# A gated attention and ternary feed-forward kernel: a new order of the calls in the lists of all five engines

## The reference

```python
xn = layernorm(x)                                   # over the last axis
# gated linear attention, 16 heads of 16
Q, K, V = (xn @ W.T).reshape(B, L, 16, 16)          # for each of Wq, Wk, Wv
g = clip(sigmoid(xn_heads @ gw.T), 1e-6)
Gc = exp(clip(cumsum(log(g), axis=1), -30, 30)) + 1e-6
R = silu(K @ sw.T)
S = cumsum(K V^T * R / Gc, axis=1) * Gc
attn = einsum(Q, S) @ Wo.T
# feed-forward with ternary weights and a low-rank side path
h = bitlinear(xn, w_fc) + gate * (xn @ v.T @ fast_b.T @ u.T)
ffn = bitlinear(relu(h) ** 2, w_proj)
out = x + attn + ffn
```

## Time and profile before

| | |
|---|---|
| median of 3 runs | 629.18 us (629.05 to 629.48) |
| span of the profiled execution, first to last instruction | 625.7 us |
| median less span: what lies around the instructions | 3.4 us |
| PE busy | 607.1 us (97%), 8246 matmuls |
| DVE busy | 533.2 us (85%) |
| ACT busy | 439.1 us (70%) |
| POOL busy | 420.3 us (67%) |
| share of the 16 transfer engines' time, by the two large queues | 56.1% and 11.7% |

### The profile page before, as it was taken

How to read it: one execution, slowest core, us unless ns; L and a number is a source line. 1 busy time by engine, 2 the same in 40 slices (tenths; PEclk the granted TensorE clock), 3 DMA queues, 4 the chain that set the end, 5 groups by cost and what they waited for, 6 DMA issues and landing times.

```text
span 625.7 us, 22751 instructions
## 1 busy us (share of the span) xinstructions
PE 607.1 (97%) x8246; PEld 529.6 (85%) x8246; DVE 533.2 (85%) x1247; ACT 439.1 (70%) x1036; POOL 420.3 (67%) x561
## 2 busy tenths in 40 slices
PE   7779999999999999999999999999999999999997
PEld 7668788888888888888888888888888888888876
DVE  6888989988888888988888889888888998888774
ACT  3687667676877667687766767776677777766763
POOL 3996667667756666676666677666666776667574
PEclk7999999999999999999999999999999999999999
DMA  9476567687667775766777677678867786667451
GB/s 292 117 167 147 128 161 178 180 167 171 146 166 182 168 182 154 153 164 160 176 159 180 182 150 152 163 175 174 161 179 158 161 158 169 176 146 165 125 79 35
DMA packets 175167, 100.24 MB, mean 160 GB/s; under 512 B 122944, under 2 KB 158144, under 8 KB 175056
## 3 DMA queue, kind: packets, MB, share of 16 engines
q1 hardware_dynamic: 151600, 79.64, 56.1%
q10 hardware_dynamic: 23456, 19.15, 11.7%
HBM read 12.49 MB, written 8.39 MB: 33 GB/s over the span
## 4 chain that ended last, share of the span: by engine, by line
PE 84%; DVE 5%; DMA 4%; POOL 3%; issue 2%; ACT 1%; SPq 1%; ACTq 0%; DVEq 0%; POOLq 0%
PE y_bank L2541 17%; PE hid_b L2512 8%; PE hid_a L2512 8%; PE attn_bank L2480 8%; PE front_b L2395 7%; PE y_bank L2556 7%; PE front_b L2354 7%; PE front_a L2376 6%; PE attn_bank L2491 4%; PE score_b L2452 3%; PE score_a L2430 2%; PE hid_b L2514 2%; PE score_b L2430 2%; PE hid_a L2514 2%; DMA relu_sq<-in_w_fc 2%
## 5 line engine op out<-in xcount | busy, mean ns | idle before, releaser
L2541 PE MATMUL y_bank<-wproj_t,sq_h 128*128 128x256 f16 x504 | 117.7, 274 | 0.4 <-DVE sq_l L1945 0.4
L2541 PE MATMUL y_bank<-wproj_t,sq_l 128*128 128x256 f16 x504 | 117.1, 273 | 0.0
L746 POOL TENSOR_TENSOR state_diag<-state,state_mask 128x256 f32<-128x256 f32 x56 | 43.1, 769 | 108.5 <-DVE state L1921 83.0
L1183 ACT ACTIVATE sq_h<-relu_sq 128x512 f16<-128x512 f32 x128 | 77.6, 627 | 54.5 <-DVE chunk_sums L1831 53.8
L1945 DVE TENSOR_TENSOR sq_l<-relu_sq,sq_h 128x512 f16<-128x512 f32 x128 | 89.2, 715 | 2.4 <-ACT relu_sq L1192 1.8
L1192 ACT ACTIVATE relu_sq<-relu_sq 128x512 f32<-128x512 f32 x128 | 79.5, 622 | 3.7 <-DVE chunk_sums L1831 2.8
L2512 PE MATMUL hid_b<-xt,wfc_t 128*128 128x256 f16 x512 | 73.4, 273 | 0.0
L2512 PE MATMUL hid_a<-xt,wfc_t 128*128 128x256 f16 x512 | 73.3, 273 | 0.0
L698 POOL TENSOR_TENSOR v_all<-vg,write 128x256 f32<-128x256 f32 x64 | 56.0, 877 | 22.2 <-DVE write L1871 22.0
L1903 DVE TENSOR_TENSOR masked<-score_b,causal_two 128x512 f32<-128x512 f32 x96 | 65.5, 682 | 2.2 <-PE score_b L2436 2.0
L1903 DVE TENSOR_TENSOR masked<-score_a,causal_two 128x512 f32<-128x512 f32 x96 | 65.3, 680 | 0.8 <-PE score_a L2430 0.5
(11 more groups left out here) (232 smaller groups left out, 1692.1 us busy)
## 6 DMA issues: line engine op xcount, KB each, us to landing
k_diag<-k SPq DMA_DIRECT2D x256, 128.0 KB, 3.4
q_stack<-q SPq DMA_DIRECT2D x128, 128.0 KB, 2.1
out_y<-y_both ACTq DMA_DIRECT2D x31, 256.0 KB, 4.3
x_sb<-in_x ACTq DMA_DIRECT2D x29, 256.0 KB, 3.5
relu_sq<-in_w_fc ACTq DMA_DIRECT2D x1, 1024.0 KB, 10.9
pj_nat<-in_w_proj ACTq DMA_DIRECT2D x1, 1024.0 KB, 12.9
k<-k_tok SPq DMA_TRANSPOSE x64, 2.8
x_sb<-in_x SPq DMA_DIRECT2D x3, 256.0 KB, 3.9
```

Of the source, the lines that this page charges most:

```text
L1183: nc.scalar.activation(sq_h[:, q], relu[:, q % 2], ACT.Square).then_inc(sq_h_done, 1)
L2541: last = mm(out_part(b, u, c), part[:, q, at:at + P], wproj_t[:, 2 * q + i], start=(q == i == n == 0 and (c == 0 or last_of_all(b, u))), s ...
```

## The change

Only the lists are changed: `prologue()`, `slot()` and `epilogue()` of each engine. Every function and every wait inside them stays, and every call of a unit is still made once. The single call that is gone is one `keep_warm(6)` on PE (12 matmul records of the trace). In the slot of PE, `values` and `carried` of chunk 0, `state_updates` and `values` of chunk 1 now stand together at the end of the slot for U2; `carried` of chunk 1 stays where it was, near the start of the next slot. The other lists shift their steps to match: the gates' logarithms, `sums_taken` and `clip_log` are made for U3 and no longer for U2, all `mask` calls of U2 are in one slot, `load` is for U6. The prologue runs correspondingly further ahead.

The slot of PE, and the parts of the others that are spoken of below:

```diff
 # tensor
             def slot(b, u):
-                values(*nxt, 0)
                 projected(b, u, 0)
-                cumulate(*after)
-                scores(*nxt, 1, 2)
-                hidden(*nxt, 1)
-                carried(*nxt, 0)
-                state_updates(*nxt)
-                queries_t(*unit_after(b, u, 3))
-                values(*nxt, 1)
                 projected(b, u, 1)
                 carried(*nxt, 1)
-                keys(*unit_after(b, u, 3))
-                projected(b, u, 2)
+                hidden(*nxt, 1)
                 hidden(*nxt, 2)
                 values_gates(*unit_after(b, u, 3), 0)
-                projected(b, u, 3)
+                projected(b, u, 2)
                 scores(*after, 0, 0)
                 scores(*after, 0, 1)
+                values_gates(*unit_after(b, u, 3), 1)
+                projected(b, u, 3)
                 attn_projected(b, u)
-                values_gates(*unit_after(b, u, 3), 1)
+                hidden(*nxt, 3)
+                cumulate(*unit_after(b, u, 3))
                 scores(*after, 0, 2)
-                hidden(*nxt, 3)
+                hidden(*after, 0)
                 scores(*after, 1, 0)
+                queries_t(*unit_after(b, u, 4))
                 scores(*after, 1, 1)
-                hidden(*after, 0)
+                scores(*after, 1, 2)
+                keys(*unit_after(b, u, 4))
+                values(*after, 0)
+                carried(*after, 0)
+                state_updates(*after)
+                values(*after, 1)
 # tensor, start of the prologue
                 keep_warm(6)
                 group_sums()
-                keep_warm(6)
+                rank_products()
                 keys(0, 0)
-                rank_products()
                 queries_t(0, 0)
-                keep_busy(6)
                 values_gates(0, 0, 0)
                 values_gates(0, 0, 1)
+                queries_t(0, 1)
+                keep_busy(6)
                 reach_row()
-                queries_t(0, 1)
-                cumulate(0, 0)
                 rank_weights(0)
                 fc_weights(0)
-                keys(0, 1)
                 rank_weights(1)
                 values_gates(0, 1, 0)
                 fc_weights(1)
                 fc_weights(2)
+                cumulate(0, 0)
                 fc_weights(3)
-                values_gates(0, 1, 1)
+                keys(0, 1)
                 scores(0, 0, 0, 0)
                 scores(0, 0, 0, 1)
+                values_gates(0, 1, 1)
 # vector, start of the prologue
                 scalars_of(0, 0)
+                refine_rstd(0, 0)
                 row_maxima()
-                refine_rstd(0, 0)
...
+                proj_scales()
                 keys_low(0, 0)
-                proj_scales()
-                values_low()
                 queries_low(0, 0)
                 stats_of(0, 2)
-                rank_rows()
                 waits_for_stats(0, 2)
                 moments_of(0, 2)
+                scalars_of(0, 2)
+                values_low()
+                stats_of(0, 3)
+                waits_for_stats(0, 3)
+                moments_of(0, 3)
+                rank_rows()
                 hidden_reach()
-                dens(0, 0)
-                stats_of(0, 3)
-                log_low(0, 0)
-                scalars_of(0, 2)
-                z_low(0, 0)
-                sums_taken(0, 0)
                 hidden_scales()
                 queries_low(0, 1)
+                dens(0, 0)
+                fc_lows(1)
                 refine_rstd(0, 2)
-                fc_lows(1)
+                log_low(0, 0)
+                sums_taken(0, 0)
+                z_low(0, 0)
                 rank_low(0)
                 rank_low(1)
-                keys_low(0, 1)
-                clip_log(0, 0)
                 mask(0, 0, 0, 0)
 # scalar, start of the prologue
                 proj_sums()
-                xt_high(0, 1)
+                queries_high(0, 0)
                 keys_high(0, 0)
                 keys(0, 0)
+                queries_full(0, 0)
+                load(1, 1)
                 values_high()
-                z_norms()
-                queries_high(0, 0)
-                queries_full(0, 0)
+                xt_high(0, 1)
                 values_gates(0, 0, 0)
```

More of the change, by code:

```diff
@@ L1220, in slot @@
-                squares(*nxt, 1)
-                values_gates(*unit_after(b, u, 3), 1)
+                decay_exp(*after)
+                squares_high(*nxt, 0)
+                queries_full(*unit_after(b, u, 3))
+                keys(*unit_after(b, u, 3))
+                rectified(*nxt, 1)
+                decay_transposed(*nxt)
+                values_gates(*unit_after(b, u, 3), 0)
+                squares(*nxt, 0)
+                rectified(*nxt, 2)
+                values_gates(*unit_after(b, u, 3), 1)
@@ L1980, in slot @@
                 nxt, after = unit_after(b, u, 1), unit_after(b, u, 2)
-                dens(*after)
-                mask(*nxt, 1, 0)
-                mask(*nxt, 1, 1)
-                log_low(*after)
-                sums_taken(*after)
-                mask(*nxt, 1, 2)
-                squares_low(b, u, 1)
-                z_low(*after)
-                carry_state(*nxt, 0)
-                refine_rstd(*unit_after(b, u, 4))
-                squares_low(b, u, 2)
-                squares_low(b, u, 3)
@@ L2005, in slot @@
+                stats_of(*unit_after(b, u, 5))
+                write_factors(*after)
+                queries_low(*unit_after(b, u, 3))
+                keys_low(*unit_after(b, u, 3))
+                waits_for_stats(*unit_after(b, u, 5))
+                move_rows(*after, 0)
+                moments_of(*unit_after(b, u, 5))
+                squares_low(b, u, 3)
                 mask(*after, 0, 0)
                 mask(*after, 0, 1)
+                move_rows(*after, 1)
+                dens(*unit_after(b, u, 3))
@@ L2007, in slot @@
+                squares_low(*nxt, 0)
+                scalars_of(*unit_after(b, u, 5))
+                log_low(*unit_after(b, u, 3))
                 scale_y(b, u)
                 unit_out(*nxt)
+                sums_taken(*unit_after(b, u, 3))
                 mask(*after, 0, 2)
+                mask(*after, 1, 0)
+                refine_rstd(*unit_after(b, u, 5))
+                mask(*after, 1, 1)
+                mask(*after, 1, 2)
+                squares_low(*nxt, 1)
+                z_low(*unit_after(b, u, 3))
@@ L2161, in prologue @@
                 sums_taken(1, 0)
-                mask(0, 3, 1, 2)
-                squares_low(0, 2, 2)
-                refine_rstd(1, 2)
+                stats_of(1, 3)
+                waits_for_stats(1, 3)
+                carry_state(0, 3, 0)
+                moments_of(1, 3)
+                scalars_of(1, 3)
                 z_low(1, 0)
-                carry_state(0, 3, 0)
-                squares_low(0, 2, 3)
+                queries_low(1, 1)
+                refine_rstd(1, 3)
+                clip_log(1, 0)
@@ L2182, in prologue @@
+                write_factors(1, 0)
+                scale_y(0, 2)
+                dens(1, 1)
+                mask(1, 0, 0, 2)
+                log_low(1, 1)
+                unit_out(0, 3)
+                sums_taken(1, 1)
+                mask(1, 0, 1, 0)
+                mask(1, 0, 1, 1)
+                mask(1, 0, 1, 2)
+                move_rows(1, 0, 0)
                 move_rows(1, 0, 1)
-                mask(1, 0, 0, 2)
+                carry_state(1, 0, 0)
+                squares_low(0, 3, 2)
@@ L2655, in prologue @@
-                values(0, 1, 0)
                 scores(0, 1, 1, 2)
+                hidden(0, 1, 3)
+                keys(0, 3)
                 carried(0, 1, 0)
-                keys(0, 3)
                 state_updates(0, 1)
-                hidden(0, 1, 3)
                 values(0, 1, 1)
-                projected(0, 0, 3)
+                attn_projected(0, 0)
                 carried(0, 1, 1)
-                attn_projected(0, 0)
+                scores(0, 2, 0, 0)
+                hidden(0, 2, 0)
@@ L2665, in prologue @@
                 values_gates(0, 3, 0)
-                scores(0, 2, 0, 0)
+                hidden(0, 2, 1)
+                values_gates(0, 3, 1)
+                projected(0, 1, 0)
                 scores(0, 2, 0, 1)
-                projected(0, 1, 0)
-                values_gates(0, 3, 1)
+                projected(0, 1, 1)
+                queries_t(1, 0)
                 scores(0, 2, 0, 2)
-                hidden(0, 2, 0)
                 scores(0, 2, 1, 0)
-                queries_t(1, 0)
@@ L2693, in prologue @@
-                hidden(0, 2, 3)
-                scores(0, 3, 0, 2)
-                hidden(0, 3, 0)
                 scores(0, 3, 1, 0)
```

636 lines of the change are left out of this document (316 added, 320 removed).

## The result

Over all timed executions the changed kernel takes 626.29 us (622.08 to 629.29, 20 runs) against 628.25 us (627.04 to 629.48, 20 runs) of the kernel before: a ratio of 0.9956, 95% interval 0.9937 to 0.9976, so 2.8 us faster by the ratio. The medians are 2.0 apart, and neither number is a typical difference: the times of the changed kernel fall in two groups, eight of 20 between 622.1 and 623.2 us and eleven between 626.1 and 629.3, so its median lies at the lower edge of the second. Forecast were 627.5 us and a gain of 1.7. The profiled execution has a span of 624.6 us, 1.1 less than before; 1.6 less was forecast. The gain is small in all and made of large terms of both signs.

What follows compares the result with a forecast made beforehand. PE was taken to bound the four stages without a gap. Terms -6.8 (PE's work), +5.4 (start), +0.8 (moved block), -0.5 (middle), -0.5 (end) sum to -1.6: span 625.7 to 624.1, plus 3.4 gives 627.5 us; range 623.8 to 632.0.

Steps and rivals of the forecast that it cites:

- The slots: PE's 27 slots: 20 save 0.14 us and 7 save 0.44, together 5.9; a slot takes 18.1 us, not 18.33.
- The four priced calls: values, carried, state_updates and values in PE's slot: 2.93 us with their entries before, 2.79 after, 0.14 saved.
- Counting changes of shape alone: PE's slots: six changes a unit before, four after, each about 0.11 us: 0.22 a unit, about 9 us in all.
- No wait in the slots: PE in the slots: the new order runs without a gap, with half a microsecond to spare in three places.
- The rival with a wait in each slot: New wait at scores(1,2) for its mask; 0.25 us a slot gives 634.3 us; chance 0.18.
- The start: Prologue to PE's first scores: 3.0 us from the order plus 2.4 from the clock, 5.4 us lost.
- I take 2.4 of 1.9 to 4.4: PE's prologue: half clock from near 28.8 us, behind a 6 us gap, costs 2.4 us.
- the 3.0 of the forecast: Prologue: the new order brings the first mask near 42.3 us in place of 39.30, 3.0 later.
- The rival with a 0.12: Start: clock falls earlier too, keys(0, 0) and queries_t(0, 0) cost 1.3 us more each; 630.1 us; chance 0.12.
- The middle of the prologue: From 37 to 118 us: DVE has as much ahead of PE; 0.5 us less waiting, within 3 either way.
- no idle time of PE after about 120 us: Sign that would show the forecast right: PE runs the slots without idle time after about 120 us.
- the 3.4 us "around" the span: Whole kernel: 3.4 us added to the forecast profiled span of 624.1 to give the forecast time, 627.5.

Runs made afterwards that it cites:

- warm: Changed kernel with keep_warm(6) added ahead of rank_products and keep_busy(26) ahead of values_gates(0,0,0) in PE's prologue: 620.30 us, ratio 0.9876 to the kernel before.
- the other run with the fillers: Changed kernel plus keep_warm(6), keep_busy(26), carried of chunk 0 behind values of chunk 1, and ScalarE issuing stack_queries(1,1): 617.98 us, ratio 0.9838.
- b_values_up: Kernel before with values of chunk 1 moved up right behind state_updates, queries_t following both, in PE's slot: 622.46 us, ratio 0.9910.
- warm6: Changed kernel with keep_warm(6) alone put back ahead of rank_products; idle time ahead of values_gates(0,0,0) stays: 624.12 us, ratio 0.9937 to the kernel before.
- after_again: The changed kernel itself, unaltered, timed again beside the kernel before: 627.1 us, ratio 0.9978.
- graft: Changed kernel with the first part of all five engines' prologue lists in the old order, slots and remaining prologue new: 619.70 us, ratio 0.9875.
- carried_last: Changed kernel with carried of chunk 0 moved behind values of chunk 1 in PE's slot: 620.49 us, ratio 0.9885 to the kernel before.
- fill: Changed kernel with keep_busy(16) added directly before values_gates(0,0,0) in PE's prologue: 623.16 us, ratio 0.9932 to the kernel before.

## Why the prediction was right, and where its steps were off

**The slots: right.** The distances are those forecast (0.80, 0.64, 0.47, 0.77), the slot 18.11 (18.1 forecast), the one that begins a batch row 17.32 (17.4). Over four slots that is 71.42 us in place of 72.59, 0.29 a slot where the terms gave 0.215: 7.9 us in the 27 slots in place of 5.9. The four priced calls gained the forecast 0.14 a slot (2.92 us with their entries before, 2.78 after). The rest is small and elsewhere, for instance `projected` ahead of `attn_projected` costs 0.79, ahead of `scores` 0.87; the prediction took such neighbours as free. That the cause is the change of shape was shown by moving one call: 0.24 a slot when a wide call divides the narrow ones, 0.24 gained in the old order when they meet. It is not the change between 16-bit and 32-bit products: `carried` of chunk 1, which is 32-bit and stands between 16-bit calls, takes 0.45, and the same call ahead of the narrow `state_updates` 0.54.

**Counting changes of shape alone** would have given 9 us. A change costs 0.09 us going in and 0.12 going out, by the distances of this trace, but `carried` directly behind a narrow call pays 0.10 more, so that the new order gained 0.14 and not 0.22 a unit from this source. The Trainium skill (TensorEngine Tiling (Array Packing), Key Properties) says that changing the mode drains TensorE. The trace shows a cost at each such change, 0.09 and 0.12 us, and so agrees; the page has no price for it.

**No wait in the slots: right.** From 145 to 588 us PE had none. The rival with a wait in each slot was no idle thought: the move of 1.3 us in the old order brought it about, 0.95 us a slot.

**The start: the size failed, and the term that failed is the clock.** "I take 2.4 of 1.9 to 4.4" was for the gap alone, with full clock until "near 28.8". With the clock held (warm) the first `scores` come at 40.1, so that the order costs 1.2 against the 3.0 of the forecast, or 3.9 in the other run with the fillers. From `keys(0, 0)` to the first `scores`, six profiles of the new order with the gap of 7 us open take 25.9 to 26.7 us, two with it filled 21.7 and 22.4, and four of the old order at full clock 20.4 (the fifth, b_values_up, with its spell of half clock, 21.7). So the clock costs 3.5 to 5 us where 2.4 was taken, and the order 1.3 to 2 where 3.0 was. The rival with a 0.12, half clock for `keys` and `queries_t` too, is what the changed kernel does: `keys` takes 2.53 us to the next call in both its profiles, and `queries_t` lasts 2.77 and 2.45. That the `keep_warm` that is gone is the cause was shown by warm6, where `keys` takes 1.32 again. The rival would have given 630.1 in all.

**The clock and the gap.** That half clock follows the gap was read rightly from the earlier trace rows. Gaps of 3.3 and 6.9 us ahead of `values_gates(0, 0, 0)` were both followed by half clock; filled to 0.6 and 1.1 us, it stayed full. For shorter gaps the length alone doesn't decide it. At 37 us of the old order PE waits for POOL, in the kernel before (first row) and in b_values_up (second):

```profile
37.21 0.22 PE L2291 MATMUL y_bank<-ident,sq_h 128*128 128x128 f16 x1 [2.18 <-POOL sq_h L822]
37.02 0.25 PE L2291 MATMUL y_bank<-ident,sq_h 128*128 128x128 f16 x1 [1.99 <-POOL sq_h L822]
```

The clock from 36 to 40 us is 1.00 in the first and 0.63 in the second. In the first slots a wait of 2.68 us was followed by half clock (warm6) and one of 2.45 was not (after_again). And in the earlier trace rows it came behind 1.4 us of idle time in two pieces. What makes the difference is open. The Trainium skill (TensorE: Matmul & The Clock Gate, HAM oscillation) warns of gaps of idle PE, and the trace agrees.

**The middle of the prologue: -3.7 where -0.5 stood.** The step argued that DVE has as much to do ahead of PE as before. It looked at DVE's load (70.1 us now, 72.7 before) and not at which of PE's waits go. The waits that went can be read from the rows. Of 4.5 us idle between the first `scores` and 118 us before, 2.6 stand ahead of `cumulate`, which waits for the logarithm that DVE's `log_low` writes:

```profile
46.26 0.19 PE L2408 MATMUL front_a<-log,causal 128*128 128x64 f16 x1 [0.99 <-DVE log L1817]
65.95 0.19 PE L2408 MATMUL front_a<-log,causal 128*128 128x64 f16 x1 [1.12 <-DVE log L1817]
102.28 0.19 PE L2408 MATMUL front_a<-log,causal 128*128 128x64 f16 x1 [0.48 <-DVE log L1817]
```

The changed kernel has none of them and graft 0.3 us; both have the new lists in this stretch, which make the logarithms further ahead. Shown is that 2.1 of the 3.7 us stay with the old start; that it is these waits is read from the profiles, and no run moved `cumulate` or the logarithms alone.

**The first slots: +3.9 where nothing stood.** "So I take no wait in the slots" was worked out for a slot in its steady state and carried to the first one, where the lists of SP and ACT first have to run a unit further ahead. This is the step that failed outright, and with it the sign "no idle time of PE after about 120 us".

**The total came out by luck.** The middle (3.2 us better than its term) and the first slots (3.9 worse) cancel, and so do PE's work with the rest of the slots (1.7 better) and the start (1.6 worse); within the start the clock was dearer and the order cheaper than taken. This is why the time came out within 1.2 us of the forecast. Even that distance is in part the base: the 3.4 us "around" the span are a median of three executions less the span of another. In every execution on record with both numbers the time is 1.8 to 2.1 us more than the span, so a span of 624.1 stands for about 626.

**The spread.** The changed kernel's runs lie between 622 and 629 us, those of before within 2.4. A part of it is shown: by the account PE lost between 0.4 and 6.3 us in the first slots in the eleven profiles of kernels with the new slots. In the run with carried last it was idle 3.68 us there, and the clock fell behind it (windows):

```profile
128.00:132.00 4.00, 1.93 (x18) 1.47 (x16) 0.61 (x2) 2.93 (x5) 1.40 (x3) 0.99 1.08 236
132.00:136.00 4.00, 2.39 (x11) 1.50 (x12) 3.41 (x10) 0.66 (x2) 2.90 (x4) 0.50 1.21 156
```

The mean granted clocks of the 20 executions point the same way: the eight below 624 us have 0.983 to 0.986, and seven of the twelve above have 0.981 or less. Another part is when `keys(0, 0)` starts: 18.4 to 20.7 us in the new order, 18.3 to 18.7 in the old. Why was not found.

## What to carry to other kernels

Price a reordering of a saturated engine by the distance between the first matmuls of neighbouring calls, for each pair of neighbours; for the calls that were priced this was good to hundredths. Then walk through the seam between prologue and loop by itself: a loop that works a unit further ahead needs its transfers and loads a unit earlier, and the queues that have slack in the loop may have none there. And before moving a call on one engine, look at who reads its result in an in-order list: 1.3 us of delay at `state_updates` cost 0.95 us a slot, while moving its neighbour instead gained 0.24.

## What the hardware showed that was not expected

- A change between the narrow shape (128\*32) and the wide one costs PE 0.09 us going in and 0.12 going out; a 32-bit product of the whole array directly behind a narrow one costs 0.10 more.
- Half clock is no local price. It came behind every gap of 3.3 us and more (fill 3.31, carried_last 3.68, the changed kernel 6.93), behind one of 1.99 (b_values_up) and not behind one of 2.18 (before) in the same place of the list. Filling idle PE with 64 matmuls that nobody reads gained 5 to 6 us of 627, a part of which can be a shorter wait in the first slots.
- A transfer's issuing on SP is no constant: one transpose took 1.25 us in most places and 4.01 at 122 us, eight key transfers 5.0 to 8.1. The same load of x landed after 2.9 us in one order and after 5.1 to 8.9 in the other.
